# A hand-ordered transformer block on one Trainium2 core: 28 of 32 batches put into a hardware loop of two

## The chip, the core and the metric

One Trainium2 (trn2) core runs the kernel. A core has five engines that each run their own instruction text and wait for each other by semaphores: PE (matmuls, with weight loads shown apart as PEld), DVE (vector work), ACT (activations), POOL (further vector work) and SP, which here only issues DMAs. The metric is the device time of one execution in microseconds. Three runs of the kernel before took 5776.75, 5777.46 and 5774.27 us: median 5776.75.

## What is computed

32 batches of 512 tokens with 256 features pass through one block. All batches do the same.

```
mod = silu(c) @ wmod                       # six rows of 256 per batch: sa, ca, ga, sb, cb, gb
h   = layernorm(x) * (1 + ca) + sa
    xn = layernorm(h) * ln1_w + ln1_b
    attention: 16 heads of 16, causal, softmax, @ o_w
    state space: xz = xn @ in_proj; conv of 4 taps, silu; dt = softplus(...)
        h_t = exp(dt_t * A) * h_(t-1) + (x_t * dt_t) * B_t     # 512 channels x 16 states
        y_t = C_t . h_t;  (y + x * D) * silu(z) @ ssm_out_w
    h = h + alpha * attention + (1 - alpha) * state space
    h = h + gelu(layernorm(h) @ ffn_w1) @ ffn_w2
x = x + ga * h
x = x + gb * (base linear + top-2 of 8 low-rank experts, on layernorm(x) * (1 + cb) + sb)
```

## The kernel before

Weights, masks and the modulation rows of all batches are prepared once. Then each engine walks through 32 batches. What an engine does in a batch is a list of named steps, written by hand in the table ORDER, one list per engine. A sign ahead of a name shifts it by a batch: `+xt0` in the list of batch n is step xt0 of batch n + 1, and `-f2_0` is f2_0 of batch n - 1. So three batches overlap at any time. `drive` takes an engine's list and calls `step` for each name, first for the steps that come ahead of batch 0, then 32 turns, then the rest.

The names that matter here:
- dec0 to dec63 (ACT, L699), scan0 to scan63 (DVE, L1192), fill0 to fill31 (POOL, L575), c and pc (DVE L1200, POOL L562), add (PE, L931): the state space part. A scan needs its decay from ACT and its input from POOL; the product with C goes to PE, which adds it up. There are two buffers for decays and eight for states, so the engines follow each other closely.
- rb0 to rb31 and rc0 to rc31 (SP, L429): DMAs of one row of B or C, spread over 128 partitions, into four slots.
- ld0 to ld3 (SP, L472 to L479): seven DMAs of queries and keys for four heads. mt: four rows of maxima through a DMA.
- mx, st, pv (PE): scores for the maxima, scores again for the exponentials, and attention times values.
- xt, qk, xs, v, z, dt, f1, f2, h2t, h3t, out (PE and a reader each): the dense parts.

Semaphores are never reset. A `Signal` has a count per batch; a step waits for `b.at(signal, n)`, which is batch x per + n. `Batch(reg, off)` can stand for a batch whose number is in a register: its index is then reg x 2 + off, and `at` gives an expression of that register. In the kernel before, every Batch has reg None, so each wait compares with a number and each DMA has a fixed address, and the whole program is straight text. `Bank` remembers who frees each of PE's four banks pM; its `into_loop` and `out_of_loop` are there and not called.

Of the kernel before, what the change touches and what calls it, by code (L numbers as in the profile page):

```python
# [18 lines left out]
B, L, D = 32, 512, 256  # L19
# [110 lines left out]
def adaln_block(nc: bass.Bass, d, out):  # L130
    ctx = ExitStack()
    with ctx:
# [223 lines left out]
        def drive(eng, order, step, banks=()):  # L356

            def turn(b, first, last):
                for name, shift in order:
                    if not (first and shift < 0 or last and shift > 0):  # L360
                        step(name, b.next(shift))

            for name, shift in order:
                if shift > 0:
                    step(name, Batch(None, 0))
            for n in range(B):
                turn(Batch(None, n), n == 0, n == B - 1)
            for name, shift in order:
                if shift < 0:
                    step(name, Batch(None, B - 1))  # L370
# [6 lines left out]
        def _(sp):  # L377
# [54 lines left out]
            def step(name, b):  # L432
# [69 lines left out]
                elif name == "put":  # L502
                    b.wait(sp, o_fin)
                    sp.dma_start(out[b.index].rearrange("(t p) f -> p t f", p=P), nrm(b)).then_inc(out_done.sem, 16)

            drive(sp, ORDER["SP"], step)
            sp.wait_ge(out_done.sem, 16 * B)
            sp.wait_ge(hres_out.sem, 16 * B)
# [6 lines left out]
        def _(pool):  # L515
# [124 lines left out]

            pool.wait_ge(built, BUILT)
            drive(pool, ORDER["POOL"], step)


        @block.scalar
        def _(act):
# [62 lines left out]
            def step(name, b):  # L709
# [146 lines left out]
                elif name == "axt":  # L856
                    b.wait(act, axt_ps)
                    act.activation(axT(b), pM[bank_of(name)][:], ACT.Copy).then_inc(axt_ok.sem, 1)

            drive(act, ORDER["ACT"], step)  # L860


# [598 lines left out]
```

## Time and profile before

| | |
|---|---|
| time, median of 3 | 5776.75 us |
| profiled execution | 5776.75 us, span on the core 5774.9 us |
| instructions | 94558 |
| busy: PE / DVE / POOL / ACT | 90% / 88% / 73% / 71% |
| granted clock of PE, mean | 0.97 |
| DMA | 812 MB, mean 141 GB/s |

The span divides into start-up, 32 like batches that overlap, and an end. The page's table of 40 slices shows the same picture from the second slice to the last but one: PE and DVE at 8 or 9 tenths, the others at 6 or 7. A time such as 3277.75 is microseconds from the span's start. The stretches quoted below are from one pair of batches in the middle of the run. Idle time of an engine is shown in brackets with what released it; the instructions that only wait or compute a register are not among the rows.

### The profile page before, as it was taken

What the parts mean: (1) busy time and instruction counts of PE and PEld (TensorE: products, weight loads), DVE (VectorE), ACT (ScalarE), POOL (GpSimd) and SP (SyncE); (2) the same over time, 40 slices, a digit from 0 to 9 for tenths busy, and PEclk for the clock granted to TensorE, in tenths of its full rate; (3) what the DMA queues carried; (4) which work ended last, traced back from release to release, by engine and by line L of the source; (5) the groups of instructions that cost most, each with busy time, mean ns of one, the idle gap of its engine ahead of it and who ended that gap; (6) DMA issues with size and microseconds to landing.
All of it is one profiled execution on the core that took longest, in us unless ns stands there. A gap on an engine that the chain in (4) does not pass through costs nothing. (4 is left out here: it accounts for less than half of the span.)

```text
span 5774.9 us, 94558 instructions
## 1 busy us (share of the span) xinstructions
PE 5203.4 (90%) x32280; PEld 3503.5 (61%) x32280; DVE 5100.7 (88%) x7776; ACT 4096.5 (71%) x6407; POOL 4188.8 (73%) x2545
## 2 busy tenths in 40 slices
PE   4799999999999999999999999999999999999986
PEld 2466666566666566666666666666666666656664
DVE  3898999999999999999999999999998998998983
ACT  3667777767777767777767777767777767777763
POOL 3677777777777777777777777777777777777772
PEclk7899999999999999999999999999999999999997
DMA  4444454444454444454444554444554444554441
GB/s 123 135 138 147 141 160 144 141 138 140 145 161 142 144 138 138 147 158 142 146 135 138 152 154 145 145 135 138 151 155 147 140 135 143 151 155 142 140 124 34
DMA packets 521455, 812.22 MB, mean 141 GB/s; under 512 B 80432, under 2 KB 227288, under 8 KB 520976
## 3 DMA queue, kind: packets, MB, share of 16 engines
q1 hardware_dynamic: 513072, 805.79, 47.0%
q8 instruction: 259, 4.24, 0.3%
q14 instruction: 220, 1.80, 0.1%
q10 hardware_dynamic: 7904, 0.39, 0.1%
HBM read 716.50 MB, written 88.38 MB: 139 GB/s over the span
## 5 line engine op out<-in xcount | busy, mean ns | idle before, releaser
L575 POOL TENSOR_TENSOR state<-scan_in,bc 128x1024 f32<-128x1024 f32 x1024 | 2404.0, 2361 | 661.0 <-PE pY L931 517.5
L1192 DVE TENSOR_TENSOR_SCAN pD<-pD,state 128x512 f32<-128x512 f32 x1536 | 1851.2, 1216 | 168.4 <-POOL state L575 103.5
L699 ACT ACTIVATE pD<-scan_in,A 128x512 f32<-128x512 f32 x2048 | 1399.0, 690 | 630.9 <-DVE state L1200 543.7
L931 PE MATMUL pY<-ident,state 128*128 128x128 f32 x8192 | 1202.7, 280 | 101.8 <-DVE state L1200 94.6
L931 PEld LDWEIGHTS pY<-ident,state 128*128 128x128 f32 x8192 | 922.5, 144 | 324.7 <-DVE state L1200 147.6
L1200 DVE TENSOR_TENSOR state<-pD,bc 128x512 f32<-128x512 f32 x1536 | 1022.9, 679 | 17.7
L1250 DVE TENSOR_REDUCE mx<-pM 128x1 f32<-128x512 f32 (+3 forms) x1408 | 849.5, 629 | 71.7 <-PE pM L1021 67.5
L800 ACT ACTIVATE region<-pM 128x512 f32<-128x512 f32 (+1 forms) x1408 | 733.2, 556 | 240.4 <-PE pM L1039 211.7
L562 POOL TENSOR_TENSOR state<-state,bc 128x512 f32<-128x512 f32 x512 | 643.1, 1272 | 275.1 <-DVE state L1192 258.7
L1037 PE MATMUL pM<-region 98*128 98x512 bf16 (+3 forms) x2048 | 529.8, 308 | 95.9 <-ACT region L800 39.9
L1192 DVE TENSOR_TENSOR_SCAN state<-pD,state 128x512 f32<-128x512 f32 x512 | 605.0, 1206 | 10.2 <-ACT pD L699 10.0
L1019 PE MATMUL pM<-region 96*128 96x512 bf16 (+3 forms) x2048 | 539.4, 312 | 78.9 <-DVE mx L1250 69.0
L1082 PE MATMUL pM<-w_f,scan_in 128*128 128x256 f32 x2048 | 458.3, 383 | 5.8 <-ACT scan_in L841 5.7
L1073 PE MATMUL pM<-region,w_f 128*128 128x512 f32 x1024 | 455.2, 598 | 2.3 <-ACT region L832 1.0
L1082 PEld LDWEIGHTS pM<-w_f,scan_in 128*128 128x128 f32 x2048 | 386.6, 191 | 64.0 <-ACT scan_in L841 14.0
L953 PE MATMUL pM<-region,vt 128*17 128x512 f32 (+3 forms) x4096 | 357.6, 438 | 48.2 <-issue 23.9
L1037 PEld LDWEIGHTS pM<-region 98*128 98x128 bf16 x2048 | 203.0, 100 | 325.9 <-ACT region L800 138.4
L1021 PE MATMUL pM<-mask_qk,identb 128*128 128x128 bf16 x2048 | 400.1, 224 | 0.0
L1039 PE MATMUL pM<-identb,mask_qk 128*128 128x128 bf16 x2048 | 397.7, 222 | 0.0
L1019 PEld LDWEIGHTS pM<-region 96*128 96x128 bf16 x2048 | 204.4, 100 | 207.4 <-DVE mx L1250 119.2
L1073 PEld LDWEIGHTS pM<-region,w_f 128*128 128x128 f32 x1024 | 190.3, 191 | 226.7 <-issue 209.3
L1232 DVE SCALAR_TENSOR_TENSOR xc<-pM,conv_w,xc 128x511 f32<-128x511 f32 (+2 forms) x384 | 286.4, 746 | 12.7 <-ACT xc L759 1.5
(171 smaller groups left out, 8318.2 us busy)
## 6 DMA issues: line engine op xcount, KB each, us to landing
bc<-bc_d SPq DMA_DIRECT2D x2048, 256.0 KB, 4.2
region<-qk_d SPq DMA_DIRECT2D x640, 128.0 KB, 4.2
qk_d<-qkp SPq DMA_DIRECT2D x64, 384.0 KB, 2.5
qk_d<-ht SPq DMA_DIRECT2D x64, 384.0 KB, 3.5
xt<-in_x_dram SPq DMA_DIRECT2D x32, 512.0 KB, 5.7
hres_d<-xt SPq DMA_DIRECT2D x32, 512.0 KB, 5.7
region<-qk_d SPq DMA_DIRECT2D x256, 64.0 KB, 3.8
x<-hres_d SPq DMA_DIRECT2D x32, 512.0 KB, 5.9
```

Source lines behind the costliest of these rows:

```text
L562: nc.gpsimd.tensor_tensor(slot, slot, bc[:, e // JP % BC_SLOTS, 1, :], ALU.mult).then_inc(pp_ok.sem, 1)
L575: nc.gpsimd.tensor_tensor(state[:, at_:at_ + JP], us[:, parity(b), k // N * JP:(k // N + 1) * JP, :], bc[:, k % BC_SLOTS, 0, :].unsqueeze( ...
L699: act.activation(pD[DECAY_BANK[e]][:], dts[:, parity(b), j], ACT.Exp, scale=A[:, j, n:n + 1]).then_inc(a_ok.sem, 1)
L800: act.activation(probs[kb % 2][:, h:h + heads, 0:n], pM[bank_of(name)][:, 0:heads * n].rearrange("p (h t) -> p h t", h=heads), ACT.Exp, sc ...
L931: ins = pe.matmul(y_part(t, e % JP), state[:, e % RING, t * P:(t + 1) * P], ident[:], is_transpose=True, start=False, stop=(e % PASS >= PA ...
L1019: pe.matmul(ps[:, s * n:(s + 1) * n], q[0:QK_ROWS, h, qb * P:(qb + 1) * P], kk[0:QK_ROWS, h, 0:n], start=True, stop=False, skip_group_chec ...
L1037: pe.matmul(ps[:, i * n:(i + 1) * n], kk[0:QK_ROWS + 2, h + i, kb * P:(kb + 1) * P], q[0:QK_ROWS + 2, h + i, kb * P:L], start=True, stop=F ...
L1073: ins = pe.matmul(ps[:], w_f1[:, k, f * P:(f + 1) * P], h2T[:, k], start=(k == 0), stop=(k == KT - 1))
L1082: ins = pe.matmul(ps[:, t * D:(t + 1) * D], gT(b)[:, f, (2 * n + t) * P:(2 * n + t + 1) * P], w_f2[:, f, :], start=(f == 0), stop=(f == FT ...
L1192: v.tensor_tensor_scan(h if e in POOL_C else decay, decay, h, 0.0, ALU.mult, ALU.add)\
L1200: v.tensor_tensor(state[:, e % RING], pD[DECAY_BANK[e]][:], bc[:, slot, 1, :], ALU.mult)\
L1250: v.tensor_reduce(mx[:, g % 2].rearrange("p (h q) -> p h q", q=TB)[:, heads[0]:heads[-1] + 1, qb], pM[bank_of(name)][:, 0:len(heads) * n]. ...
```

## The change

The 32 turns of `drive`, which Python unrolled, are now: two turns written out, a hardware loop (`Fori`) of 14 passes with two turns in its body, and two turns written out. Two turns are one pass since buffers alternate between even and odd batches. In the body a Batch carries the loop's register, so the values of its waits and the addresses of its DMAs are computed at run time. Each engine has a loop and a counter of its own; the engines don't meet at its end.

```diff
             for name, shift in order:
                 if shift > 0:
                     step(name, Batch(None, 0))
-            for n in range(B):
-                turn(Batch(None, n), n == 0, n == B - 1)
+            turn(Batch(None, 0), True, False)
+            turn(Batch(None, 1), False, False)
+            with eng.Fori(0, (B - 4) // 2) as i:
+                for bank in banks:
+                    bank.into_loop(i)
+                turn(Batch(i, 2), False, False)
+                turn(Batch(i, 3), False, False)
+            for bank in banks:
+                bank.out_of_loop(B - 4)
+            turn(Batch(None, B - 2), False, False)
+            turn(Batch(None, B - 1), False, True)
             for name, shift in order:
                 if shift < 0:
                     step(name, Batch(None, B - 1))
```

On PE, at the end of a batch's list and the start of the next, the built order before (L931 is add, L1006 is z, L1027 is mt, L1082 is f2):

```order
L1019 MATMUL pM<-region 128x128
L1021 MATMUL pM<-mask_qk,identb 128x128
L931 MATMUL pY<-ident,state 128x128 [waits p_ok]
L931 MATMUL pY<-ident,state 128x128 x3
L1006 MATMUL pM<-w_in,xnT 128x512 [waits xt_ok,mx_ok]
L1006 MATMUL pM<-w_in,xnT 128x512
L1027 MATMUL pM<-ident,mx 16x128 [waits mx_ok]
```

and at the same place now, the end of the loop's body first and then its start (all lines behind L363 have moved by nine):

```order
L1030 MATMUL pM<-mask_qk,identb 128x128
L89 REGISTER_ALU
L940 MATMUL pY<-ident,state 128x128 [waits p_ok]
L940 MATMUL pY<-ident,state 128x128 x3
L368 REGISTER_ALU
L368 COMPARE_AND_BRANCH
...
L368 ISA
L89 ISA [waits mx_ok]
L1015 MATMUL pM<-w_in,xnT 128x512 [waits xt_ok]
L1015 MATMUL pM<-w_in,xnT 128x512
L89 REGISTER_ALU
L1036 MATMUL pM<-ident,mx 16x128 [waits mx_ok]
```

The matmuls stand as before; a branch and register instructions (REGISTER_ALU is one operation, ISA on L89 and L368 several in one) have come between them.

On SP, at rc22 and the start of a batch's list (rb22, rb25, rb23, ld3), before:

```order
L429 DMA bc<-bc_d 128x512 [waits p_ok]
L429 DMA bc<-bc_d 128x512 [waits b_ok] x3
L472 DMA region<-qk_d 32x1x2048 [waits t_ps]
L474 DMA region<-qk_d 32x1x2048
L472 DMA region<-qk_d 32x1x2048
```

and now, in the body:

```order
L368 ISA
L438 ISA [waits b_ok]
L438 DMA bc<-bc_d 128x512
L89 REGISTER_ALU
L438 ISA [waits b_ok]
L438 DMA bc<-bc_d 128x512
L89 REGISTER_ALU
L438 ISA [waits b_ok]
L438 DMA bc<-bc_d 128x512
L89 ISA
L481 ISA [waits t_ps]
L481 DMA region<-qk_d 32x1x2048
```

The wait has moved from the DMA to a register instruction ahead of it, which computes the DMA's address once the wait is over.

## Rows read from the trace of the kernel before

**Rows 1.** The page's span and busy time: us (share of the span), instructions.
```profile
span 5774.9 us, 94558 instructions
PE 5203.4 (90%) x32280; PEld 3503.5 (61%) x32280; DVE 5100.7 (88%) x7776; ACT 4096.5 (71%) x6407; POOL 4188.8 (73%) x2545
```

**Rows 2.** Three stretches: us; busy PE, PEld, DVE, ACT, POOL; PE clock, DMA share, GB/s.
```profile
3252.00:3272.00 20.00, 20.00 (x110) 15.94 (x109) 19.85 (x30) 10.64 (x19) 15.28 (x12) 1.00 0.68 193
3292.00:3310.00 18.00, 18.00 (x89) 14.64 (x87) 11.14 (x22) 13.79 (x16) 13.72 (x11) 1.00 0.47 133
3350.00:3400.00 50.00, 43.97 (x321) 26.52 (x320) 49.73 (x70) 37.04 (x63) 32.10 (x18) 0.97 0.59 175
```

**Rows 3.** Timeline of ACT and DVE at ACT's z0: start, us, engine, instruction.
```profile
3252.83 0.61 ACT L787 ACTIVATE zs<-pM 128x512 f32<-128x512 f32 x1
3253.30 0.71 ACT L699 ACTIVATE pD<-scan_in,A 128x512 f32<-128x512 f32 x1
3254.38 1.22 DVE L1192 TENSOR_TENSOR_SCAN pD<-pD,state 128x512 f32<-128x512 f32 x1
```

**Rows 4.** Timeline of POOL and DVE around POOL's fill8.
```profile
3268.89 7.00 POOL L575 TENSOR_TENSOR state<-scan_in,bc 128x1024 f32<-128x1024 f32 x3
3275.52 2.32 DVE L1192 TENSOR_TENSOR_SCAN pD<-pD,state 128x512 f32<-128x512 f32 x2
```

**Rows 5.** Timeline of DVE from c16; in brackets idle time before and its releaser.
```profile
3277.75 1.26 DVE L1200 TENSOR_TENSOR state<-pD,bc 128x512 f32<-128x512 f32 x2
3300.51 1.23 DVE L1192 TENSOR_TENSOR_SCAN pD<-pD,state 128x512 f32<-128x512 f32 x1 [3.02 <-POOL state L575]
```

**Rows 6.** Timeline of PE at add18, z3 and f2.
```profile
3291.19 0.61 PE L931 MATMUL pY<-ident,state 128*128 128x128 f32 x4
3291.63 1.88 PE L1006 MATMUL pM<-w_in,xnT 128*128 128x512 f32 x4
3294.06 7.17 PE L1082 MATMUL pM<-w_f,scan_in 128*128 128x256 f32 x32
```

**Rows 7.** Timeline of SP's queue at rb22, and POOL's fill that reads it.
```profile
3180.03 0.54 SPq L429 DMA_DIRECT2D bc<-bc_d  x1
3185.12 0.79 SPq L429 DMA_DIRECT2D bc<-bc_d  x2
3189.04 2.35 POOL L575 TENSOR_TENSOR state<-scan_in,bc 128x1024 f32<-128x1024 f32 x1 [1.48 <-PE pY L931]
```

**Rows 8.** Instruction queues: packets, MB, time as a share of 16 engines.
```profile
q8 instruction: 259, 4.24, 0.3%
q14 instruction: 220, 1.80, 0.1%
```

**Rows 9.** DMA issues: count, KB each, median us from issue to landing.
```profile
bc<-bc_d SPq DMA_DIRECT2D x2048, 256.0 KB, 4.2
region<-mrow SPq DMA_DIRECT2D x256, 4.0 KB, 1.8
```

**Rows 10.** Timeline of PE's weight loads, attention times values.
```profile
2809.34 0.13 PEld L953 LDWEIGHTS pM<-region,vt 128*17 128x17 f32 x8 [0.16 <-issue]
```

**Rows 11.** The page's costliest groups: the transposing matmuls of add.
```profile
L931 PE MATMUL pY<-ident,state 128*128 128x128 f32 x8192 | 1202.7, 280 | 101.8 <-DVE state L1200 94.6
```

**Rows 12.** Timeline of POOL at start-up and in the last layer norm.
```profile
5.62 0.20 POOL L534 MEMSET region<- 128x128 f32 x1
5.97 0.29 POOL L535 TENSOR_SCALAR_AFFINE_SELECT region<-region 128x128 f32<-128x128 f32 x1
5741.46 1.02 POOL L545 TENSOR_TENSOR ln_rs<-ln_rs,mhalf 128x4 f32<-128x4 f32 x1
5742.56 0.20 POOL L548 TENSOR_TENSOR ln_nm<-ln_nm,ln_rs 128x4 f32<-128x4 f32 x1
```

**Rows 13.** Timeline of DVE, short links of the routing weights.
```profile
5752.95 0.19 DVE L1319 TENSOR_REDUCE esum<-top 128x4 f32<-128x32 f32 x1
5753.18 0.18 DVE L1321 RECIPROCAL esum<-esum 128x4 f32<-128x4 f32 x1
```

## The prediction

> **What bounds the kernel now.** I read the page's busy line first [rows 1]. PE is busy 5203 of 5775 us and DVE 5101, so two engines are near full and neither alone is the bound. Busy shares say only that; which of the two ends last changes within a batch. The table of stretches shows it [rows 2]. From 3252 to 3272 us PE has no idle time (20.00 of 20) and DVE hardly any (19.85). From 3292 to 3310 PE is again full (18.00 of 18) while DVE is idle 18.00 - 11.14 = 6.9 us. From 3350 to 3400 it is the other way: DVE 49.73 of 50, PE 43.97. So a stop of PE before 3310 has nothing to hide behind, and a stop of DVE just before 3292 has 6.9 us.
>
> Next I look at where the change's new points fall. Each engine's text gets its branch at the same place of its own order, once in two batches: ACT between yt3 and z0, POOL between fill7 and fill8, DVE between scan17 and c16, PE between add18 and z3, SP between rc22 and rb22. In time these are apart: ACT at 3252.83 [rows 3], POOL at about 3271.2 (the second of the three multiplications that start at 3268.89) [rows 4], DVE at 3277.75 [rows 5], PE at 3291.6 [rows 6], and SP at 3180.03, some 70 us before the others [rows 7]. They don't fall together, so each is priced by itself.
>
> **The change, part by part.** The work, its order and the number of DMAs stay as they are. Three things are new.
>
> *1. The branch back, 14 times on each engine.* The program of before is one straight text. It comes in over two instruction queues, 259 and 220 packets, 4.24 + 1.80 MB [rows 8]; 6.04 MB over 94558 instructions [rows 1] is 64 bytes each, so every instruction is fetched once. The body on PE is long: 2 x 2 x 32280 / 32 = 4035 matmuls and weight loads [rows 1] and some 390 waits and register instructions, 0.28 MB or 17 packets of 16 KB. Unless an engine keeps so much text, the branch leads to text that has to be fetched again, and the engine stops once what is queued has run. No row of before shows such a stop. I bound the fetch by two transfers: 4 KB land 1.8 us after their issue, the 256 KB of a row of bc 4.2 us [rows 9]. A packet of 16 KB itself took about 0.3% x 16 x 5774.9 / 259 = 1.1 us [rows 8]. I take 3.0 us, the middle of 1.8 and 4.2. Queued work shortens it: eight weight loads start within 0.13 us [rows 10], so eight pairs of load and matmul had been lying ready. Short pairs start 0.11 us apart (four take 0.61 [rows 6], one 0.28 [rows 11]: 0.33 over three), so eight are 0.9 us. A stop is then 3.0 - 0.9 = 2.1 us; I take it for every engine but SP, which executes what it issues and has no such stock.
>
> The Trainium skill says the same of the mechanism: in "Runtime: NRT & Kernel Launch", section "Instruction fetch mechanics", the prefetch is sequential, and a taken branch to text outside the window waits for a DMA of the target page. No row of before shows a branch back, so none bears this out yet.
>
> Where the stops land:
> - PE, 2.1 us at 3291.6: PE is full around it, and the 32 matmuls at 3294.06 (f2) make the last product of the batch before, for which DVE waits [rows 2, 6]. All of it counts: 2.1.
> - ACT, 2.1 us at 3252.83: the next decay (0.71 us from 3253.30, done at 3254.01) is read by the scan at 3254.38 [rows 3], so 0.4 us are slack and DVE is 1.7 late. DVE has its 6.9 us later, but before them stand the sum and the layer norm for which PE's f1 waits. Between none and all I take half: 0.85.
> - DVE, 2.1 us at 3277.75: until 3292 PE works through f1, which doesn't wait for DVE, and after that DVE is idle 6.9 us, 3.02 of it in one wait for POOL [rows 2, 5]. Hidden: 0; without that cover it would be 2.1.
> - POOL, 2.1 us at 3271.2: a third of the 7.00 us is 2.3, so this fill ends at 3273.6 and its scan starts at 3275.52, 1.9 us later [rows 4]. The 0.2 left over falls under DVE's cover: 0.
> - SP, 3.0 us at 3180.03: the load after it was issued at 3185.12 in any case; the late one lands at 3180.03 + 3.0 + 4.2 = 3187.2, and the fill that reads it starts at 3189.04 [rows 7, 9]. 0.
>
> Sum 2.95 us a turn, x 14 = 41 us. Bounds: below, 0 (the fetch hides); above, 4.2 us with no queued work, all of it on PE, all but 0.4 on ACT, half on DVE: 4.2 + 3.8 + 2.1 = 10.1 a turn, 141 us.
>
> *2. Register instructions ahead of waits.* A wait that compared with a number now compares with a register, which must be computed. In the built order a body of two batches holds 294 register instructions on PE, 306 on DVE, 311 on ACT, 132 on POOL and 342 on SP. A price from POOL's start-up [rows 12]: the selection at 5.97 starts 0.15 us after the memset before it ends (5.62 + 0.20), with a register move between; a plain link at 5742.56 starts 0.08 after its predecessor's end (5741.46 + 1.02). That makes about 0.07 us. Per batch it is 147 x 0.07 = 10.3 us of PE's sequencer and 10.7 of DVE's. It runs while the engine works on what was handed to it, so it shows only behind short instructions: DVE's links of 0.19 us start every 0.23 us [rows 13]. There are a dozen a batch (routing, layer norms). I let five of them be 0.07 late: 0.35 us a batch, x 28 batches = 10 us. Lower bound 0; upper bound all of PE's, 10.3 x 28 = 288 us.
>
> *3. DMAs whose address is computed.* 342 register instructions stand among 232 DMAs on SP, one of them often between the wait and the DMA. That makes a load 0.07 to 0.14 us later, on a queue whose loads mostly land well before they are read. Taken as 0, and bounded by 0.14 us on each of 5 loads a batch that something waits for, 0.7 x 28 = 20 us. A gain is not among the bounds: no instruction, transfer or wait goes away.
>
> Sum: 41 + 10 = 51 us. The profiled execution took 5776.75 us (span 5774.9), which is also the median of the three runs: 5776.75 + 51 = 5828 us, 0.9% slower.
>
> **The rivals.**
> *A, the fetch is hidden (not slower).* Place: the sequencer of PE at the branch. If it runs ahead of its engine by the whole fetch, the 2.1 us become 0, and ACT's likewise. It decides at a stock of 3.0 us, where I counted 0.9. For it: f1's matmuls are long, and eight of those lying ready would be over 3 us. Against: at add18, just before the branch, pairs are short (0.61 us for four) [rows 6]. Time: 5777 and register work of 0 to 10 us: 5777 to 5787.
>
> The skill's "Advanced Engine Details and Errata", section "Engine Queue Depths", gives TensorE 64 entries and the other engines 8. By it 32 pairs at 0.11 us would be 3.5 us, more than the fetch: PE's stop would be 0 and the sum 5777 + 12 + 10 = 5799. No row here shows more than eight pairs ready.
>
> *B, a stop costs more.* If the queue runs dry before the branch is taken, nothing of the fetch is covered: PE 3.0, ACT 3.0 - 0.4 = 2.6 in full, DVE half of 3.0, 7.1 x 14 = 99 us, and 10: 5886. For it: from 3252 to 3272 DVE and PE are both full [rows 2], so a delay of one can cost the other. Against: the 6.9 us of DVE behind it.
>
> *C, register work is exposed.* Were a quarter of PE's 10.3 us a batch exposed instead of the 0.35, 72 us would stand in the place of 10: 5890; all of it, 6106. Against: the pairs that lay ready [rows 10].
>
> *D, a gain.* Nothing is taken away; only if a stop shifts the engines into a better phase could it come out under 5765.
>
> **How the numbers follow.** Measurements of this kernel can tell about 0.2%, 11.6 us, from no change. Forecast (5789 to 5870) 0.57; A 0.13; B 0.19; C 0.08; D 0.03. The range leaves out A, D and the far part of C: 5786 to 5920. Faster 0.03 (D), within 0.2% 0.13 (A), slower 0.84.
>
> **What the profile after will show.** Right: the same counts of matmuls, activations and DMAs; on each engine a gap of 1 to 4 us once in two batches, at z3, z0 and decay 5, c16, fill8 and rb22, in which nothing is waited for; busy times unchanged. The two batches of a turn then take some 3.6 us more, the first two and the last two batches nothing. Wrong: no gap at the branch (A); gaps of 3 us and more with DVE's waits grown (B); a tenth of a microsecond at every wait (C); far fewer than 479 instruction packets, which would mean that bodies are kept.

## The result and the profile after

The changed kernel takes 5942.22 us (median of 4 runs, 5938.76 to 5949.41). Beside it the kernel before took 5776.68 (4 runs, 5774.27 to 5777.46). The ratio is 1.0287, with a 95% interval of 1.0272 to 1.0302. The loop costs 165.5 us. I had forecast 51 and a range up to 5920. The direction was right; the size was three times too small, and the time lies outside the range.

The page of the changed kernel, first rows and instruction queues:

```profile
span 5938.9 us, 115651 instructions
PE 5262.0 (89%) x32280; PEld 3518.1 (59%) x32280; DVE 5103.3 (86%) x7776; ACT 4094.7 (69%) x6407; POOL 4194.8 (71%) x2545
...
q8 instruction: 296, 4.85, 0.3%
q14 instruction: 454, 3.72, 0.2%
```

The counts are those of [rows 1]. DVE, ACT and POOL are busy for the same time within 6 us, so the loss is idle time there. PE alone is busy 58.6 us longer with the same 32280 matmuls; this turns out to matter. The instruction packets grew from 479 [rows 8] to 750: text is fetched again in each pass. Not all of the growth is the branches': straight text with the same register instructions (e1 below) already takes 274 + 355 = 629 packets, so 121 come with the branches.

Where does the time go? PE around its branch (start, us, engine, instruction, idle time before), in two passes one behind the other:

```profile
3384.38 0.22 PE L1030 MATMUL pM<-mask_qk,identb 128*128 128x128 bf16 x1
3384.44 0.60 PE L940 MATMUL pY<-ident,state 128*128 128x128 f32 x4
3390.23 3.49 PE L1015 MATMUL pM<-w_in,xnT 128*128 128x512 f32 x4 [5.19 <-issue]
3393.56 0.27 PE L1036 MATMUL pM<-ident,mx 128*16 128x128 f32 x1
...
3749.94 3.77 PE L1015 MATMUL pM<-w_in,xnT 128*128 128x512 f32 x4 [5.91 <-issue]
```

L940 is add18 and L1015 is z3, which started in the kernel before at 3291.63 without a gap and took 1.88 us [rows 6]. Now PE stands for 5.19 us, and z3 takes 3.49. "<-issue" says that PE waited for nothing that the profile shows. The pass is 3749.94 - 3390.23 = 359.7 us long; in the kernel before the same stretch is 3638.43 - 3291.63 = 346.8, so this one costs 12.9. The body runs 14 times, but only 13 of the branches are taken: behind the last one, which falls through, no engine stops (PE's gap there is 0.00 us). So the loop costs 165.5 / 13 = 12.7 us a taken branch, registers included.

The table of stretches by the microsecond shows both halves of that (columns as in [rows 2]: busy PE, PEld, DVE, ACT, POOL; PE clock, DMA share, GB/s):

```profile
3384.00:3385.00 1.00, 1.00 (x14) 0.80 (x11) 1.00 (x2) 1.00 (x1) 1.00 (x1) 1.00 0.50 146
3386.00:3387.00 1.00, 0.00 (x0) 0.00 (x0) 0.83 (x1) 1.00 (x1) 1.00 (x1) 1.00 1.04 357
3388.00:3389.00 1.00, 0.00 (x0) 0.00 (x0) 0.96 (x6) 0.00 (x0) 1.00 (x1) 1.00 0.97 322
3389.00:3390.00 1.00, 0.00 (x0) 0.00 (x0) 0.28 (x4) 0.00 (x0) 1.00 (x3) 0.94 0.16 54
3390.00:3391.00 1.00, 0.77 (x1) 0.50 (x2) 0.00 (x0) 0.00 (x0) 1.00 (x2) 0.50 0.11 33
3392.00:3393.00 1.00, 1.00 (x3) 0.39 (x2) 0.00 (x0) 0.00 (x0) 1.00 (x1) 0.50 0.00 0
3394.00:3395.00 1.00, 1.00 (x8) 0.90 (x7) 0.00 (x0) 0.98 (x2) 1.00 (x1) 1.00 0.00 0
```

While PE stands, the DMA engines are full (share 1.04 and 0.97). The granted clock falls late in the microsecond from 3389 to 3390, when PE has been idle since 3384.44 + 0.60 = 3385.04; when PE starts again it is 0.50, the lower level of 1.2 GHz, and it is back at 1.00 from 3393.3, 3.1 us after z3's start. At this place the clock was 1.00 in the kernel before [rows 2].

The other engines' stops in the changed kernel, each at its own branch (ACT z0, DVE c16, POOL fill8 and fill9):

```profile
3344.73 0.60 ACT L796 ACTIVATE zs<-pM 128x512 f32<-128x512 f32 x1 [2.45 <-issue]
```

```profile
3371.53 1.29 DVE L1209 TENSOR_TENSOR state<-pD,bc 128x512 f32<-128x512 f32 x2 [2.16 <-issue]
```

```profile
3363.70 4.67 POOL L584 TENSOR_TENSOR state<-scan_in,bc 128x1024 f32<-128x1024 f32 x2 [0.91 <-issue]
```

These are near the gaps of 1 to 4 us that I had forecast. PE's is not.

### The profile page after: what moved, and what is told of

Same layout as the page of the kernel before. It is cut to its first block and busy times, and to the rows that moved or that the text cites. A ratio compares the mean times of both kernels' runs of the same rounds, so it can differ in the third digit from the quotient of the medians.

```text
span 5938.9 us, 115651 instructions
## 1 busy us (share of the span) xinstructions
PE 5262.0 (89%) x32280; PEld 3518.1 (59%) x32280; DVE 5103.3 (86%) x7776; ACT 4094.7 (69%) x6407; POOL 4194.8 (71%) x2545
## 5 line engine op out<-in xcount | busy, mean ns | idle before, releaser
L940 PE MATMUL pY<-ident,state 128*128 128x128 f32 x8192 | 1214.0, 282 | 102.9 <-DVE state L1209 94.8
L940 PEld LDWEIGHTS pY<-ident,state 128*128 128x128 f32 x8192 | 928.6, 145 | 335.7 <-DVE state L1209 145.8
L1082 PE MATMUL pM<-region,w_f 128*128 128x512 f32 x1024 | 460.1, 600 | 18.1 <-ACT scan_in L846 14.2
L1015 PE MATMUL pM<-w_in,xnT 128*128 128x512 f32 x512 | 277.0, 668 | 96.0 <-issue 67.0
L1082 PEld LDWEIGHTS pM<-region,w_f 128*128 128x128 f32 x1024 | 189.5, 191 | 248.1 <-issue 210.5
```

The costliest lines, as they stand in the source:

```text
L940: ins = pe.matmul(y_part(t, e % JP), state[:, e % RING, t * P:(t + 1) * P], ident[:], is_transpose=True, start=False, stop=(e % PASS >= PA ...
L1082: ins = pe.matmul(ps[:], w_f1[:, k, f * P:(f + 1) * P], h2T[:, k], start=(k == 0), stop=(k == KT - 1))
```

## The experiments

All ran against the kernel before on the same chip; "+n us" is the difference of the two medians. They answer four questions: is it the branch or the registers (e1, e2, e3, e10, e11), which engine's (e4 to e8, e12), does the place decide (e9, e13, e14), and why does PE stop longer than the others (e15 to e18).

### Registers or branch

**e1.** No loop: 32 turns of straight text, but the waits and addresses of the 28 middle batches come from a register.

```diff
-            with eng.Fori(0, (B - 4) // 2) as i:
+            counter = nc.alloc_registers(...)
+            nc.regs_mov(counter, 0)
+            for k in range((B - 4) // 2):
+                i = nc.snap(counter, min_val=0, max_val=(B - 4) // 2 - 1)
                 ... (the banks)
                 turn(Batch(i, 2), False, False)
                 turn(Batch(i, 3), False, False)
+                nc.regs_alu(counter, counter, 1, op=ALU.add)
```

> All 32 batches written out again, without a branch, but 28 of them with the waits and addresses computed from a register, as in the loop. Theory 1 (the 166 us are stops behind the branch; register work is hidden): 5777 to 5797 us. Theory 2 (register instructions, and on SP the work between wait and DMA, cost the larger part): 5860 to 5940 us.

5796.34 us, +21; ratio 1.0036 (1.0021 to 1.0050). The register work costs 21 us, or 0.8 a batch; I had said 10. That leaves 165.5 - 21 = 144 us for the branch.

**e2.** The changed kernel, with a hint for the back edge. In the trace it is an instruction BRANCH_PREFETCH_HINT at the head of each pass, on every engine (ACT's first at 473.22 us, 348 us before the branch that it is for).

```diff
-            with eng.Fori(0, (B - 4) // 2) as i:
+            with nc.Fori(0, (B - 4) // 2, engines=OrderedEngineSet([eng.engine]), hint_back_edge=True) as i:
```

> The loop as in the change, with a hint at the head of each body that lets the engine fetch the branch's target ahead of time. Theory 1: the stops at the branch (5.4 us on PE, 2.6 on ACT, 1.9 on DVE, 4.1 on SP in the changed kernel's trace) shrink to under 1 us each, and the time falls to 5780 to 5830 us. Theory 2: at most the stops of PE go, 5880 to 5930 us. If the hint does nothing, 5942.

5796.77 us, +22; ratio 1.0037 (1.0023 to 1.0051). That is e1's time with the loop in it. PE around its branch (add18 and z3):

```profile
3300.52 0.61 PE L941 MATMUL pY<-ident,state 128*128 128x128 f32 x4
3300.97 1.88 PE L1016 MATMUL pM<-w_in,xnT 128*128 128x512 f32 x4
```

No gap, and z3 takes 1.88 us again. The instruction packets are 638, nearly those of e1. So the 144 us are the wait for text behind a taken branch and what follows from it, and nothing else of the loop.

**e3.** Four batches in the body, 7 passes, of whose branches 6 are taken (an index and a wait's value step by four batches instead of two, which the cut below leaves out).

```diff
-            with eng.Fori(0, (B - 4) // 2) as i:
+            with eng.Fori(0, (B - 4) // 4) as i:
                 turn(Batch(i, 2), False, False)
                 turn(Batch(i, 3), False, False)
+                turn(Batch(i, 4), False, False)
+                turn(Batch(i, 5), False, False)
```

> Loop body of four batches, seven passes: half the branches, the same number of register instructions. Theory 1: half of the 166 us stays, 5855 to 5865 us. Theory 2: register work stays whole, over 5900 us.

5862.60 us, +88; ratio 1.0158 (1.0141 to 1.0175). 21 + 144 x 6 / 13 = 87: the cost goes with the number of taken branches, not with the text in the body.

### Which engine

e4 to e8 loop on one engine and leave the others straight; e12 loops on all but PE.

```diff
+            if eng.engine in (mybir.EngineType.PE,):
+                (the loop)
+            else:
+                for n in range(B):
+                    turn(Batch(None, n), n == 0, n == B - 1)
```

**e4, PE alone.**

> The loop on PE alone; the other four engines are written out as before. Theory 1: 14 stops of 5.4 us of a PE that is full at that place, 60 to 80 us, so 5837 to 5857 us. Theory 2: PE's register work is the least exposed, and the stop overlaps other waits, under 5815 us.

5872.82 us, +98; ratio 1.0171 (1.0154 to 1.0188). Without the 3 us of e10 below these are 95 / 13 = 7.3 us a taken branch where I had 2.1, the largest error of the prediction. z3 in e4:

```profile
3349.34 3.78 PE L1019 MATMUL pM<-w_in,xnT 128*128 128x512 f32 x4 [5.15 <-issue]
```

5.15 us stand before it and 3.78 - 1.88 = 1.9 us are lost in it, 7.05 together; the half clock goes on behind z3, until 3354.4.

**e5, ACT alone.**

> The loop on ACT alone. The changed kernel's trace has a stop of 2.6 us at each branch of ACT. The prediction's step (half of 1.7 us felt, 14 times): +12 us, 5787. Theory 1a (the stop is felt in full, since DVE needs the next decay 0.4 us later and PE and DVE are both full there): 14 x 2.2 = 31, and ACT's register work: 5805 to 5812.

5832.39 us, +56; ratio 1.0101 (1.0084 to 1.0118): 56 / 13 = 4.3 us a taken branch where I had 0.85. PE's z1 in the kernel before, and the same four matmuls in e5, which come behind the sum that waits for DVE:

```profile
3264.47 1.98 PE L1006 MATMUL pM<-w_in,xnT 128*128 128x512 f32 x4
```

```profile
3299.80 3.11 PE L1019 MATMUL pM<-w_in,xnT 128*128 128x512 f32 x4 [2.52 <-DVE x L1295]
```

ACT's stop (2.88 us in this pass) is passed to DVE, then to PE, which idles 2.52 us; and its clock then falls (0.88 in 3296 to 3302, 0.84 in the next 6 us). That adds 1.1 us to z1 and more behind it: from z1's start to the start of the next group of z, PE takes 3306.49 - 3299.80 = 6.69 us, and 3269.48 - 3264.47 = 5.01 in the kernel before. 2.52 + 1.68 = 4.2 is nearly the 4.3. And DVE's wait for POOL, the 3.02 us of [rows 5] that I had counted as slack, in e5:

```profile
3337.43 1.23 DVE L1205 TENSOR_TENSOR_SCAN pD<-pD,state 128x512 f32<-128x512 f32 x1 [3.02 <-POOL state L588]
```

It is still 3.02 us, and 3337.43 - 3300.51 = 36.92 us later than in the kernel before (what seven passes and this one have cost). The fill that ends it, before and in e5:

```profile
3298.12 2.36 POOL L575 TENSOR_TENSOR state<-scan_in,bc 128x1024 f32<-128x1024 f32 x1
```

```profile
3335.04 2.36 POOL L588 TENSOR_TENSOR state<-scan_in,bc 128x1024 f32<-128x1024 f32 x1
```

POOL is late by the same 36.92: what it waits for had come late as well. In both rows a wait whose releaser is late by the same delay takes nothing of it up.

**e6, DVE alone.**

> The loop on DVE alone, stop of 1.9 us at c16. The prediction's step (hidden in DVE's idle time behind it): 5775 to 5782. Theory 1a (felt in full): 14 x 1.9 = 27 us, 5802.

5796.60 us, +20; ratio 1.0038 (1.0024 to 1.0053): 20 / 13 = 1.6 us a taken branch, DVE's registers included, instead of 0, beside a gap of 1.85:

```profile
3291.41 1.29 DVE L1213 TENSOR_TENSOR state<-pD,bc 128x512 f32<-128x512 f32 x2 [1.85 <-issue]
```

DVE's idle time for POOL behind it is 3.03 us in e6, as before.

**e7, SP alone.**

> The loop on SP alone, stop of 4.1 us at rb22, and all of its register work between wait and DMA. The prediction's step (the late load still lands before its fill): 0 for the stop, 0 to 20 for the register work, 5775 to 5795. Theory 1a (the load of rb22 and those behind it make POOL late): 14 x 2 to 4 us and 10, 5810 to 5840.

5774.54 us, ratio 1.0000 (0.9990 to 1.0009). SP's stop (4.1 us from the branch to the next instruction, median) costs nothing that can be measured: its loads are early enough.

**e8, POOL alone.**

> The loop on POOL alone, stop of 3.0 us between the branch and the next instruction of its sequencer, less what is queued. The prediction's step (the fill is 1.9 us early): 5775 to 5780. Theory 1a: 14 x 2.5 = 35 us, 5810.

5793.46 us, +17; ratio 1.0034 (1.0022 to 1.0047), where I had 0. e11 divides it.

**e10, PE alone with e2's hint, and e11, POOL alone with e1's registers and no loop.**

> Loop on PE alone with the back edge hinted, which removed the stops in e2. Theory: what is left is PE's register work, at most 5 of e1's 20 us since POOL alone had 17: 5776 to 5782, so e4's +97 is all stop. Rival: PE's register work is a part of e4's cost that only shows when the other engines keep their constants, 10 to 25 us: 5787 to 5802.

> No loop anywhere; POOL alone computes the values of its waits from a register, as in e1. Theory: e8's +17 us is POOL's register work and not its stop, since its lateness grew by small steps and the fill at the branch caught up: 5790 to 5796. Rival: the stop makes it: 5776 to 5781.

e10 is 5779.84 us, +3 (ratio 1.0006, 0.9997 to 1.0016), e11 is 5785.72, +9 (1.0015, 1.0005 to 1.0025). PE, with 294 register instructions in a body, loses 3 us to them, which can't be told from nothing; POOL, with 132, loses 9. Eight of e10's ten times lie below all ten of e11, so the number of register instructions doesn't tell their price. What does is open; that POOL's waits are followed more closely is a guess that no run tests. By the medians e8's 17 are half registers and half stop, so neither side was quite right on e11; each half is known to some 6 us only.

**e12, all but PE.**

> Loops on ACT, DVE, POOL and SP, straight text on PE. Theory (the engines' stops add up, since none is given back): 56 + 20 + 17 + 0 = 93 us, 5865 to 5875; PE's 97 would then overlap with the rest by 25. Rival: the three overlap among themselves (ACT's stop and DVE's come within 30 us of each other in a turn), and PE's adds in full: 166 - 97 = 69 us, 5838 to 5850.

5850.62 us, +74; ratio 1.0124 (1.0107 to 1.0141). The rival came out (0.6 us above its range): ACT's, DVE's and POOL's costs (56 + 20 + 17) overlap by 19, and PE's 98 comes on top nearly in full (74 + 98 = 172, measured 165.5).

### Does the place decide?

**e9.** PE alone again, but the body begins and ends inside a batch, where PE waited 2.75 us for DVE.

```diff
+            cut = order.index(("add44", 0))
             turn(Batch(None, 0), True, False)
             turn(Batch(None, 1), False, False)
+            part(Batch(None, 2), order[:cut])
             with eng.Fori(0, (B - 4) // 2) as i:
                 for bank in banks:
                     bank.into_loop(i)
-                turn(Batch(i, 2), False, False)
+                part(Batch(i, 2), order[cut:])
                 turn(Batch(i, 3), False, False)
+                part(Batch(i, 4), order[:cut])
             ...
-            turn(Batch(None, B - 2), False, False)
+            part(Batch(None, B - 2), order[cut:])
             turn(Batch(None, B - 1), False, True)
```

> Loop on PE alone, as in e4, but its body begins and ends between mt2 and add44 instead of at the end of the list. The stop is the same; in the kernel before, PE waits 2.75 us for DVE at that place (add44, start 3373.72). Theory (a stop costs what it exceeds the wait that stood there, and nothing is given back later): 5.4 - 2.75 = 2.6 us a turn for the stop plus about 1 for registers, 3.7 x 14 = 52 us, so 5815 to 5840. Rival (a stop of PE costs its full length wherever it stands, since the waits that it covers move with it): 97 us as in e4, 5865 to 5880.

5794.24 us, +17; ratio 1.0032 (1.0021 to 1.0044), against +98 at the end of the list. It is better than my own estimate. The two rows of add44, before and in e9:

```profile
3373.72 0.81 PE L931 MATMUL pY<-ident,state 128*128 128x128 f32 x4 [2.75 <-DVE state L1200]
```

```profile
3381.48 1.11 PE L952 MATMUL pY<-ident,state 128*128 128x128 f32 x4 [3.50 <-DVE state L1221]
```

The idle time grew by 0.75 us only, to 3.50. So the stop at this place isn't 5.4 but 3.5 us. The clock behind it was already low in the kernel before (last columns: PE clock 0.52, DMA share, GB/s), so the longer stop had less of it to take away:

```profile
3374.00:3376.00 2.00, 2.00 (x11) 1.32 (x10) 1.93 (x4) 1.88 (x4) 0.00 (x0) 0.52 0.59 170
```

**e14, ACT alone, cut before z1**, where ACT waited 3.77 us.

> Loop on ACT alone, as in e5, cut before z1, where ACT waits 3.77 us for PE before (start 3266.49). Theory: the stop of 2.7 us lies inside that wait, only register work stays: 5777 to 5784. Rival: the stop costs the same 4.0 us a turn as in e5: 5825 to 5840.

5778.40 us, +2; ratio 1.0002 (0.9993 to 1.0012). ACT's 56 us are gone, though ACT still needs 2.4 us (median) from the branch to its next instruction.

**e13, all engines, each cut where it had waited long.**

```diff
+CUTS = {
+    "PE": ('add44', 0),
+    "Activation": ('z1', 0),
+    "DVE": ('scan24', 0),
+    "Pool": ('fill27', 0),
+}
```

> All five engines loop, as in the changed kernel, but each body is cut where its engine had a long wait in the kernel before: PE before add44 (2.75 us), ACT before z1 (3.77), DVE before scan24 (3.02), POOL before fill27 (4.75); SP as before. Theory (a stop costs only what it exceeds the wait that stood there): e1's 20 us of register work, and e9's rest of at most 14: 5793 to 5812. Rival (e9 was a matter of PE alone, the stops of ACT, DVE and POOL cost as much at any place since lateness is never given back): e12's 74 and e9's 17, about 5865.

5797.55 us, +22; ratio 1.0033 (1.0021 to 1.0045). That is e1's register work and nearly nothing else. ACT and DVE at their branches:

```profile
3279.22 0.60 ACT L805 ACTIVATE zs<-pM 128x512 f32<-128x512 f32 x1 [3.85 <-PE pM L1024]
```

```profile
3313.22 1.23 DVE L1210 TENSOR_TENSOR_SCAN pD<-pD,state 128x512 f32<-128x512 f32 x1 [3.08 <-POOL state L593]
```

The waits were 3.77 and 3.02 us without a branch in them. So the same wait for POOL that could not take up a stop 20 us or more ahead of it (e5, e6) takes up one that falls into it.

### Why PE stops longer

**e15.** PE alone, cut between f1_3 and f1_4: PE is full there, but its matmuls are long.

> Loop on PE alone, cut between f1_3 and f1_4: dense work as in e4, no wait to hide behind, but the matmuls lying ready are long (0.44 us each instead of 0.11). Theory (what lies ready, about eight pairs, runs on during the fetch): 3.5 us are covered, a stop of 5.4 becomes 2 to 3: 28 to 45 us and 3 of registers, 5808 to 5825. Rival (the branch waits until PE has nearly run dry and then fetches, so the length of the queued work does not matter): 85 to 100 us, 5862 to 5877.

5788.26 us, +12; ratio 1.0022 (1.0012 to 1.0031), better than either.

```profile
3452.00 7.11 PE L1095 MATMUL pM<-region,w_f 128*128 128x512 f32 x16
3459.53 1.98 PE L1095 MATMUL pM<-region,w_f 128*128 128x512 f32 x4 [0.43 <-issue]
```

Counted from the record of the branch, PE ran seven more pairs here, 3.5 us of work, and stood for 0.43. In the changed kernel it ran fourteen, but in 1.3 us. With 3.7 us from the branch to the next matmul, as in e9, the stock explains e15, and would leave 2.4 us at the end of the list. It doesn't leave 5.2.

**e16, PE alone, cut between mx1_8 and mx1_9**, in other short pairs.

> Loop on PE alone, cut between mx1_8 and mx1_9, another stretch of very short pairs (a start every 0.06 us) with no wait of PE near it. Theory S (in short pairs the branch is reached while its request for text is held up, so it comes 3 to 4 us after the branch as in e4): a stop of 5.4 us, 80 to 100 us in all, 5855 to 5877. Rival N (the late request belongs to the end of the list in e4; anywhere else the request comes 1.0 us after the branch as in e9 and e15, and the stop is 3.5 less about 0.5 of short pairs): 3 x 14 = 42 and 3 of registers, 5815 to 5830.

5797.09 us, +21; ratio 1.0036 (1.0022 to 1.0050). PE stands 1.3 us, less than N said, since thirteen pairs lay ready with 2.4 us of work, some of them long; 1.3 x 13 + 3 = 20.

**e17, PE alone, cut before add19**, two steps behind e4's place.

> Loop on PE alone, cut before add19, that is z3 (four matmuls of 0.44 us) and mt0 later than in e4. Theory S: z3's long matmuls stand before the branch, the request comes 1.0 us after it, and of 3.5 us some 1.9 are covered: 1.6 x 14 = 22 and 3, 5795 to 5810. Rival N (the region around the end of the list is what makes the request late): a stop of 3.5 to 5 us, 5825 to 5865.

5852.35 us, +76; ratio 1.0135 (1.0118 to 1.0152). Within N's range, against S: long matmuls before the branch, and still a gap of 3.70 us, and half the clock behind it:

```profile
3335.93 1.11 PE L953 MATMUL pY<-ident,state 128*128 128x128 f32 x4 [3.70 <-issue]
```

```profile
3336.80:3337.80 1.00, 1.00 (x5) 0.81 (x4) 0.00 (x0) 0.95 (x3) 1.00 (x1) 0.50 0.00 0
```

**e18, PE alone, cut before mt2**, at the end of 4 us of very short pairs.

> Loop on PE alone, cut one step before e9's, between mx2_10 and mt2. As in e4 the branch comes at the end of 4 us of very short pairs (3365.3 to 3369.3 in the kernel before); behind it stand waits of 1.16 and 2.75 us. Theory S2 (a long run of short pairs before the branch makes its request for text late): request 3 us or more after the branch, a stop of about 5.4 that covers the two waits but passes on some 2: 5800 to 5825. Rival N (the place at the end of the list alone): request 1.0 us after the branch, stop of 3: 5780 to 5798.

5805.11 us, +29; ratio 1.0050 (1.0033 to 1.0067).

```profile
3392.95 0.27 PE L1049 MATMUL pM<-ident,mx 128*16 128x128 f32 x1 [3.38 <-issue]
3395.61 1.11 PE L953 MATMUL pY<-ident,state 128*128 128x128 f32 x4 [2.39 <-DVE state L1222]
```

The time is in S2's range, but the trace says N: the packet of text comes 1.0 us after the branch, not 3. The waits of 1.16 (mt2) and 2.75 us (add44) of the kernel before have become 3.38 and 2.39, 1.86 more; 1.86 x 13 and 3 of registers are 27 of the 29 us. S and S2 have fallen. What is special about the end of the list shows when the DMA queues are read from the branch on (packets, MB, share of 16 engines). In e4 the first 4 us after the branch at 3342.6, and the 1.2 us behind them:

```profile
q1 hardware_dynamic: 1009, 1.04, 86.7%
```

```profile
q1 hardware_dynamic: 310, 0.30, 71.9%
q8 instruction: 1, 0.02, 4.8%
```

and in e9 and e16 the first 2.5 us after the branch:

```profile
q8 instruction: 1, 0.02, 2.7%
q1 hardware_dynamic: 29, 0.00, 0.9%
```

```profile
q8 instruction: 1, 0.02, 3.0%
```

q1 carries the data, q8 PE's text. At the end of the list SP has just issued rows of bc, x and the modulation: over a thousand data packets move before PE's packet of text, which comes 4.1 us after the branch. It doesn't wait until the burst is over: it comes at 3346.7, and the DMA engines are still 0.85 full from 3346.6 to 3347.6. Elsewhere little or nothing moves and it comes after 1.0 us. Once it has started it takes no longer in the burst (4.8% of 16 x 1.2 us = 0.9 us) than alone (2.7% of 16 x 2.5 us = 1.1 us). The medians over the 13 taken branches, counted from the record of the branch: the first packet of text, the data that moved from 0.5 to 1.5 us after the branch, the work that PE still had, and the time that it then stood:

| PE's branch | first packet, us | data, KB | work left, us | PE stands, us | cost, us |
|---|---|---|---|---|---|
| e4, end of the list | 4.0 | 156, then some 330 per us | 1.6 (16 pairs) | 5.2 | 98 |
| changed kernel, same place | 3.8 | 132, then some 330 per us | 1.3 (14) | 5.2 | a part of 165 |
| e17, add19 | 2.6 | 313, but the burst ends sooner | 1.4 (3) | 3.7 | 76 |
| e18, mt2 | 1.0 | 0 | 0.5 (6) | 3.3 | 29 |
| e9, add44 | 1.0 | 0 | 0.2 (0) | 3.5 | 17 |
| e16, mx1_9 | 1.0 | 0 | 2.4 (13) | 1.3 | 21 |
| e15, f1_4 | 1.0 | 18 | 3.5 (7) | 0.5 | 12 |

In every row first packet + 2.5 to 3 us = work left + standing. The place sets three things: how late the text comes, how much work covers it, and what stood there anyway (in e9 a wait of 2.75 us and a clock already low behind it, beside which its longer stop costs less than e16's).

The pattern holds at all places that were tried, but not within one place: in e4 the 13 packets start 2.6 to 5.0 us after the branch, behind 112 to 195 KB in the third column, and the more data doesn't go with the later packet. And no run moved the transfers and left the branch where it was. That the text is late because of the data is a reading of the traces, not shown; what sets the packet's place within a burst is open.

## Why the prediction was wrong

Point by point, by its own steps.

- *The text comes in again after a branch, and the engine stops.* Right. The packets grew from 479 to 750, 121 of them with the branches, and e2, whose branches don't wait, has no gap. The Trainium skill's rule ("Runtime: NRT & Kernel Launch", section "Instruction fetch mechanics": a taken branch outside the window waits for a DMA of the target page) agrees with the trace: PE's first packet of text starts 3.8 us after the branch, and its next matmul 6.5 us after it.
- *14 branches.* One too many: 13 are taken (e3, with 6 in the place of 13, bears it out).
- *A fetch of 3.0 us.* Near for DVE, ACT and POOL (from the branch to the next instruction 2.8 us in e6, 3.3 in e5, 3.7 in e8, medians), short for SP (4.1 in e7) and for PE where little data moves (3.7 from the branch to the next matmul in e9), and wrong where I applied it: in the changed kernel PE's next matmul comes 6.5 us after its branch. I read the fetch's duration from transfers that had been issued in calm stretches, and never looked at what the DMA engines do at the branch. The table of stretches has that column; in the kernel before the share is 1.03 from 3293 to 3294, just behind PE's new branch.
- *The stock of 0.9 us.* Near: 1.3 us. But I took it for a time of its own; it is up to 16 pairs (none in e9), whose length depends on the matmuls. The Trainium skill's "Advanced Engine Details and Errata", section "Engine Queue Depths", gives TensorE 64 entries; as an estimate from that figure, 32 pairs of 0.44 us would have covered 14 us in e15, and PE stood after 3.5. No run showed more than 16 pairs ready.
- *PE's stop of 2.1 us counts in full: 29 us.* This is the step that failed most. It counts in full, but it is 5.2 us (median; 4.0 to 6.2 over the 13), not 2.1, and behind it PE runs at half its clock, which I had at nothing: z3 takes 3.49 us for 1.88. The term should have been 95 (e4 less e10), 7.3 us a taken branch.
- *ACT's 0.85 us: 12 us.* Failed: 54 (e5 less e14). Of the stop 2.5 us reached PE, and PE's clock fell after that idle time, which cost 1.7 us more.
- *DVE 0, hidden by 6.9 us of idle time.* Failed: DVE's 20 us, registers included. The idle time was a wait within the same chain (e5: 3.02 us before, 3.02 us after, 36.92 us later). It hides only a stop that falls into it (e13).
- *POOL 0.* Wrong by some 8 us of stop, beside 9 of registers, by the medians. *SP 0.* Right (e7).
- *Register work 10 us.* A term of the right kind, at half its size: 21 (e1), nearly half of it POOL's, which I had not priced.
- *Computed addresses 0.* Right (e7).

So of the 165.5 us 21 are registers and 144 are stops, against 10 and 41. No rival reached 5942. C gave 5890 and B 5886. Of them B had the right kind of mechanism, a stop that costs more, by the wrong reason: not that nothing of the fetch is covered, but that it takes longer at this place and the clock falls behind it. A, the hidden fetch, failed at the end of the list and is all but true at f1, the very matmuls that I had named for it (e15, 0.43 us). C failed by e1, in which every register wait stands and 21 us are lost, and D did not come.

No version beats the kernel before. Two loops on all engines come within 22 us of it: the hinted back edge (e2) and the cuts (e13).

## What to carry to other kernels

A stop costs what it exceeds the wait into which it falls; idle time of the same engine 20 us later is no slack if its releaser is in the same chain, so a delay should be followed through to the releaser before a wait is counted as cover. Cut a loop's body where each engine waits anyway, or behind long matmuls; or hint the back edge. Keep it away from bursts of DMA too, if the reading of the table is right, which no run shows by itself. A gap in PE's work is to be priced with the clock behind it, which the column of granted clock shows.

## What the runs showed of the hardware that I had not expected

- With a hint at the head of each pass PE has no gap at its branch (e2: +22 us, the same as straight text with registers, +21).
- The first packet of text starts 1.0 us after PE's branch, and PE starts again 3.7 to 4.0 us after it, when little data moves (e9, e15, e16, e18; medians). Among transfers of some 200 to 360 GB/s the packet started 2.6 to 4.0 us after the branch, and PE after 5.1 to 6.7 (e17, e4, the changed kernel; medians).
- After a stop of 5.19 us PE's granted clock was 0.50 until 3.1 us into its work, and four matmuls of 512 columns took 3.49 us for 1.88. In the passes shown it was 0.50 after 3.70 us of idle time too (e17), and stayed at 1.00 after 0.43 us (e15).
- POOL's 132 register instructions in a body cost 9 us over 14 passes (e11), PE's 294 cost 3, which is within the noise (e10).
- The last branch of a loop, which is not taken, stops no engine (changed kernel: PE's gap 0.00 us behind it, against 4.0 to 6.2 behind the 13 others).
